# Seven more pairs of expert outputs loaded before the last stage, seven parts instead of six, and gathers without bounds checks, in a graph and mixture-of-experts kernel

## The chip, the cores and the metric

The kernel runs on one core of a Trainium2 chip. The metric is the device time of one execution in microseconds (us). The kernel before takes 3670.58 us (median of three runs, 3669.82 to 3671.08). TensorE multiplies matrices (PE in the profile, PEld its weight loads), VectorE is DVE, ScalarE is ACT, GpSimd is POOL and SyncE, which here only issues DMAs, is SP.

## The reference, cut to what matters

There are 12500 nodes with 256 features each. A first layer sums, for every node, the weighted features of its neighbours over 200,000 sorted edges, and multiplies by a weight matrix. The second layer is the one that the change touches. It scores every node for four experts by attention over 131,072 edges, keeps the two best, and adds up the outputs of four small networks with those gates:

```python
h = (x @ W_gat).reshape(M, HEADS, EXPERTS)
e = leaky_relu(a_src[src] + a_dst[dst], 0.2)      # one value for each edge and head
alpha = exp(e - max over dst) / sum over dst
agg = segment_sum(h[src] * alpha, dst) + b_gat
scores = layernorm(agg, gamma, beta).reshape(M, HEADS, EXPERTS).mean(1)
w = softmax(top_k(scores, 2))
for ei in range(EXPERTS):
    out += gate[ei] * (gelu(x @ W1[ei] + b1[ei]) @ W2[ei] + b2[ei])
```

The result is x plus this sum. The edges of the second layer point at nodes 0 to 8191 only, and every node has a loop to itself.

## The kernel before, in words

The nodes lie in 98 tiles of 128 (`TILES`), and two tiles are a pair (49 pairs). The edges of the second layer are sorted by destination into 128 rows of 1024 columns. The kernel has four stages, each a block in which the five engines run programs of their own, in order, and meet at the end.

`layernorm_and_plan` and `weighted_sums` compute the first layer and sort the edges. Near the end of `weighted_sums`, GpSimd starts to write one small record for each node into `adst_first`, at the node's first edge. That is `spread`, one indirect DMA for each tile (L487): 28 of them are in `weighted_sums` and 70 at the start of the next block. A node without edges has a position far beyond the table, which the DMA's bounds check drops.

`attention_and_experts` does two things side by side. TensorE, ScalarE and a part of VectorE compute the four experts of each pair and store the outputs to `y_dram` (1 MB for a pair, x and the bias already added). GpSimd gathers one record for each edge, 1024 indirect DMAs of 128 rows (L1198), in eight blocks of columns: seven of 140 and the last of 44. For each block VectorE computes running maxima and running sums (`maxima`, `messages`, `sums`), ScalarE the exponentials, and SP stores the states to `state_dram` (L1177). Seven blocks are fitted into slots between pairs, the last comes after the last pair. Then come a short exchange between the 128 rows (`carry`), a gather of one row of states (L1206), its correction and its store (L1209): this is the tail of the softmax. After the states of block 0, SP loads the pairs 0 to 3 into `ys_ahead`, long before they are used. The memset of `m.ns` (L1189) on GpSimd fills the rows of nodes without edges with zeros.

`combine` is the last stage. GpSimd gathers the final state of each node, one indirect DMA for each tile (L1615), in six parts that end at the tiles of `PART`. For a part, VectorE runs the 28 or so small operations of `gates` (L1715 to L1761), with three questions to ScalarE in between (exponential, root, exponential: `weights`, `deviation`, `gate`). Then the pairs of the part are summed. Every fourth pair (every second in the last part) is summed by VectorE (`pair`, L1772 and L1775). The others are summed by TensorE: ScalarE makes eight diagonal matrices of gates (L1644), TensorE multiplies them with the expert outputs (L1686), and ScalarE copies the sum out of PSUM (L1650). ScalarE's order is written out by hand in `summed`: four pairs of part n-1, `weights(n)`, one pair, `deviation(n)`, one pair, `gate(n)`, and the rest. SP first issues the loads of pairs 4 to 15, with three small constant loads among them, and then, in the order of the pairs, stores pair i and refills a slot with pair i-2+16 when the store of pair i-2 has landed. `SLOTS` is 16. SP's DMAs, the state stores of the stage before included, are all on its one queue, q1.

## Time and profile before

| | |
|---|---|
| median of three runs | 3670.58 us |
| the profiled execution | 3668.62 us, its span 3666.8 us |
| TensorE / VectorE / ScalarE / GpSimd busy | 81% / 56% / 22% / 74% of the span |
| mean granted TensorE clock | 0.903 of full speed |
| last stage, first gather to the end of the span | 3488.62 to 3666.8 us |

Times in rows of the trace are microseconds from the start of the span. Busy shares are averages over stages with different limits, so each stage is read by itself. A row of the timeline gives start, duration, engine, line and operation, and in brackets how long the engine was idle before it and what ended that.

### The profile page before, as it was taken

How to read it: one execution, taken by the hardware profiler on the slowest of the kernel's cores; microseconds unless marked ns; L12 is line 12 of the kernel's file. 1: busy time of each engine (PE TensorE's matmuls, PEld its weight loads, DVE VectorE, ACT ScalarE, POOL GpSimd, SP SyncE). 2: the span in 40 equal slices, each digit the busy share in tenths (PEclk: the TensorE clock that was granted, in tenths of full speed). 3: DMA queues.
4: the chain of work that ended last, by engine and by line, in shares of the span. 5: the costliest groups of instructions: out<-in, count | busy, mean ns of one | idle time of the engine just before them, and what ended most of it. 6: DMA issues, size and time to landing. Idle time of an engine off the chain costs nothing. (4 is left out here: it accounts for less than half of the span.)

```text
span 3666.8 us, 60445 instructions
## 1 busy us (share of the span) xinstructions
PE 2973.6 (81%) x13893; PEld 2432.7 (66%) x13894; DVE 2042.9 (56%) x6851; ACT 817.8 (22%) x2321; POOL 2708.2 (74%) x2817
## 2 busy tenths in 40 slices
PE   1475665666866889978888799999999999999648
PEld 1354544554645666766666688888888888888537
DVE  8777778787787676664344223343343334242567
ACT  6300000000111111211222222223232322232247
POOL 6677777777777777777777777777777777777573
PEclk6786887887877999999999899999999999999879
DMA  9643333333433444444444222242223222322289
GB/s 347 198 120 106 107 111 111 112 114 112 116 115 111 121 122 124 128 119 127 128 128 131 58 73 54 54 122 54 73 54 76 54 74 53 79 73 54 57 299 366
DMA packets 276554, 424.71 MB, mean 116 GB/s; under 512 B 59704, under 2 KB 210211, under 8 KB 275363
## 3 DMA queue, kind: packets, MB, share of 16 engines
q0 software_dynamic: 114208, 216.64, 23.6%
q1 hardware_dynamic: 64175, 114.71, 8.6%
q10 hardware_dynamic: 98004, 91.50, 7.7%
q8 instruction: 60, 0.98, 0.1%
q14 instruction: 107, 0.88, 0.1%
HBM read 317.12 MB, written 105.97 MB: 115 GB/s over the span
## 5 line engine op out<-in xcount | busy, mean ns | idle before, releaser
L672 POOL DMA_INDIRECT rows<-feats,src_t x1500 | 1446.8, 965 | 466.9 <-issue 443.6
L1198 POOL DMA_INDIRECT got<-row_dram,src_sorted x1024 | 990.0, 967 | 312.1 <-issue 312.1
L833 PE MATMUL node_sums<-rows,ys_ahead 128*128 x3904 | 989.5, 408 | 231.6 <-SPq L656 101.2
L833 PEld LDWEIGHTS node_sums<-rows,ys_ahead 128*128 128x128 f32 x3904 | 762.4, 202 | 427.5 <-issue 314.9
L1282 PE MATMUL d_hidden<-d_yt,w 128*128 128x256 f32 x3136 | 711.9, 380 | 0.8 <-DVE d_yt L1368 0.8
L1293 PE MATMUL d_expert<-w,hid 128*128 128x256 f32 x3136 | 708.7, 379 | 0.0
L1293 PEld LDWEIGHTS d_expert<-w,hid 128*128 128x128 f32 x3136 | 596.7, 190 | 80.2
L1282 PEld LDWEIGHTS d_hidden<-d_yt,w 128*128 128x128 f32 x3136 | 595.0, 191 | 79.7 <-DVE d_yt L1368 1.2
L1345 DVE TENSOR_TENSOR yo<-d_expert,x_and_b 128x512 f32<-128x512 f32 x196 | 135.5, 691 | 837.5 <-PE d_expert L1293 829.9
L892 DVE TENSOR_SCALAR ys_ahead<-iota,rel,ew_t 128x128 f32<-128x128 f32 x1952 | 557.1, 364 | 65.3 <-DVE rel L888 2.3
L1226 ACT ACTIVATE hid<-d_hidden,b1c 128x256 f32<-128x256 f32 x784 | 323.7, 471 | 983.8 <-PE d_hidden L1282 792.7
L888 DVE TENSOR_SCALAR rel<-dst_t,step_base 128x4 f32 x488 | 123.5, 253 | 508.8 <-PE node_sums L833 421.1
L725 ACT COPY edge_plan<-node_sums 128x256 f32<-128x256 f32 x98 | 36.5, 372 | 1605.2 <-PE sums_and_xc_turned L825 1605.2
L1009 DVE TENSOR_SCALAR ys_ahead<-iota_b,hist_columns 128x128 bf16<-128x128 bf16 (+1 forms) x2048 | 334.5, 279 | 2.5 <-DVE hist_columns L1005 0.2
L845 PE MATMUL counts<-ys_ahead 128*128 128x98 bf16 x1024 | 77.2, 249 | 157.9 <-DVEq L1012 157.9
L845 PEld LDWEIGHTS counts<-ys_ahead 128*128 128x128 bf16 x1024 | 67.8, 122 | 168.1 <-DVEq L1012 165.6
L1615 POOL DMA_INDIRECT edge_plan<-state_dram,last_pos x98 | 100.9, 1029 | 31.9 <-issue 29.6
L487 POOL DMA_INDIRECT adst_first<-node_dst,first_pos x98 | 97.5, 995 | 30.7 <-issue 29.6
L1686 PE MATMUL f_sum<-ys,gate_diagonals 128*128 128x256 f32 x384 | 90.7, 398 | 23.4 <-issue 12.5
L821 PE MATMUL x_product<-edge_plan 128*128 128x256 f32 x400 | 107.1, 392 | 0.0
L1686 PEld LDWEIGHTS f_sum<-ys,gate_diagonals 128*128 128x128 f32 x384 | 76.0, 200 | 38.0 <-issue 27.0
L1418 DVE TENSOR_TENSOR_SCAN got<-decay,last_state,got 128x140 f32<-128x140 f32 (+1 forms) x160 | 86.1, 538 | 4.9
(302 smaller groups left out, 2270.2 us busy)
## 6 DMA issues: line engine op xcount, KB each, us to landing
y_dram<-yo ACTq DMA_DIRECT2D x196, 256.0 KB, 2.2
ys<-y_dram SPq DMA_DIRECT2D x36, 1024.0 KB, 9.2
rows<-feats,src_t POOLq DMA_INDIRECT x1500, 2.8
got<-row_dram,src_sorted POOLq DMA_INDIRECT x1024, 2.4
ys_ahead<-y_dram SPq DMA_DIRECT2D x13, 1024.0 KB, 9.1
x_dram<-edge_plan ACTq DMA_DIRECT2D x98, 128.0 KB
d_x<-x_dram ACTq DMA_DIRECT2D x49, 256.0 KB, 3.1
ys_ahead<-in_x ACTq DMA_DIRECT2D x97, 128.0 KB
```

The source lines that it names most:

```text
L672: pool.indirect_dma_start(rows[:, g % RING, j, :], None, feats, bass.IndirectOffsetOnAxis(ap=m.src_t[:, g * GT + j:g * GT + j + 1], axis=0 ...
L833: t = pe.matmul(psA[:, ds(((code >> 1) & 1) * 512, FEAT)], hot[:, r, j, :], rows[:, ds((code >> 2) & (RING - 1), 1), j, :], start=False, s ...
L845: t = pe.matmul(psC[:, 0:TILES], hot_lo[:, q % 2, j, :], hot_hi[:, q % 2, j, :], start=False, stop=False)
L888: v.tensor_scalar(rel[:, r, :], m.dst_t[:, ds(g * GT, GT)], m.step_base[:, ds(s, 1)], None, ALU.subtract).then_inc(s_rel, 1)
L892: t = v.tensor_scalar(hot[:, r, j, :], m.iota[:], rel[:, r, j:j + 1], m.ew_t[:, ds(g * GT + j, 1)], ALU.is_equal, ALU.mult)
L1009: c.inc(v.tensor_scalar(t[:, q % 2, j, :], iota_b[:, 0:wide], col[:, q % 2, n, j:j + 1], None, ALU.is_equal))
L1198: pool.indirect_dma_start(got[:, k, j, 0:ROWF], None, m.row_dram, bass.IndirectOffsetOnAxis(ap=m.src_sorted[:, BEGIN[b] + j:BEGIN[b] + j + ...
L1226: t = act.activation(hid[:, e % 2, 2 * q + f, :], psL[(e % 2) * 2 + q][:, f, :], ACT.Gelu, bias=b1c[:, e, 2 * q + f:2 * q + f + 1])
L1282: t = pe.matmul(psL[(e % 2) * 2 + q][:, f, :], w1[:, h, e, (2 * q + f) * P:(2 * q + f + 1) * P], yt[:, k, h, :], start=(h == 0), stop=(h = ...
L1293: q = pe.matmul(psO[e % 2][:, t, :], hid[:, e % 2, f, t * P:(t + 1) * P], w2[:, f, e, :], start=(f == 0), stop=(f == FB - 1))
L1345: v.tensor_tensor(yo[:, e, :, :], psO[e % 2][:], xb[:, e, :, :], ALU.add).then_inc(s_yo, 1)
L1686: q = pe.matmul(psum[j % SUMS][:, t, :], diag[:, j % DIAGS, t, e, :], y_of(i)[:, t, e, :], start=(e == 0), stop=(e == EXPERTS - 1))
```

## The change

There are four edits. (1) SP, after it has issued the state store of block 6 and all experts' outputs are stored, loads seven pairs (5 to 11) into memory that the experts no longer need (`w1`, `w2`, `hid`, `yo`, `x_and_b2`). A fifth pair (4) goes early into the free rest of `edge_plan`. `SLOTS` becomes 17, and `combine` itself first loads the three constants and then pairs 12 to 16. (2) `PART` has seven parts instead of six. VectorE takes every third pair of a part, and still every second in the last. (3) The bounds checks of L487 and L1615 are gone. Nodes without edges point at spare rows instead, which SP fills with zeros once in `weighted_sums`. The memset L1189 goes, an iota on GpSimd and three small VectorE operations come in `weighted_sums`. (4) Three semaphores are merged into others.

```diff
-SLOTS = 16
-AHEAD = 4
+SLOTS = 17
+AHEAD = 5
+LATE = 7
...
+        m.y_slots = [m.ys_ahead[:, k] for k in range(AHEAD - 1)] + pairs_of(m.plan[:, TILES * STATE:])
+        for t in (m.w1, m.w2, m.hid, m.yo, m.xb):
+            m.y_slots += pairs_of(t[:].rearrange("p a b c -> p (a b c)"))
...
     pool.indirect_dma_start(m.adst_first, bass.IndirectOffsetOnAxis(ap=m.first_pos[:, t:t + 1], axis=0),
-                            m.node_dst[:, t, :], None, bounds_check=GEDGES - 1, oob_is_err=False
-                            ).then_inc(m.s_sc, 16)
+                            m.node_dst[:, t, :], None).then_inc(m.s_sc, 16)
...
+            c.inc(pool.iota(spare[:], pattern=[[P, TILES]], base=GEDGES, channel_multiplier=1,
+                            allow_small_or_imprecise_dtypes=True))
...
-                c.done(v.tensor_scalar(cnt[:], m.has_edges[:], -4.0 * GEDGES, 4.0 * GEDGES, ALU.mult, ALU.add))
-                c.inc(v.tensor_tensor(m.first_pos[:], pos[:, 0, :], cnt[:], ALU.add))
-                c.done(v.scalar_tensor_tensor(m.last_pos[:], pos[:, 1, :], -1.0, cnt[:], ALU.add, ALU.add))
+                c.inc(v.tensor_tensor(pos[:, 0, :], pos[:, 0, :], spare[:], ALU.subtract))
+                c.done(v.tensor_scalar(pos[:, 1, :], pos[:, 1, :], 1.0, spare[:, 0:1], ALU.subtract, ALU.subtract))
+                c.inc(v.tensor_tensor(pos[:, 0, :], pos[:, 0, :], m.has_edges[:], ALU.mult))
+                c.done(v.tensor_tensor(pos[:, 1, :], pos[:, 1, :], m.has_edges[:], ALU.mult))
+                c.inc(v.tensor_tensor(m.first_pos[:], pos[:, 0, :], spare[:], ALU.add))
+                c.done(v.tensor_scalar(m.last_pos[:], pos[:, 1, :], spare[:, 0:1], None, ALU.add))
...
                     for k in range(AHEAD):
-                        load_pair(sp, m, k, k, m.ys_ahead[:, k])
+                        load_pair(sp, m, k, k, m.y_slots[k])
+                if b == len(BLOCK_PAIR) - 1:
+                    sp.wait_ge(s_l2, PAIRS * EXPERTS)
+                    sp.wait_ge(s_yo, PAIRS * EXPERTS)
+                    for e in range(EXPERTS):
+                        sp.wait_ge(s_st[e], 16 * PAIRS)
+                    for k in range(AHEAD, AHEAD + LATE):
+                        load_pair(sp, m, k, k, m.y_slots[k])
...
-            pool.memset(m.ns, 0.0).then_inc(s_clear, 1)
...
-        PART = [0, 10, 28, 48, 68, 88, T]
+        PART = [0, 6, 18, 36, 56, 74, 90, T]
...
-                     if (i - PART[n] // 2) % (4 if n < PARTS - 1 else 2) == 0]
+                     if (i - PART[n] // 2) % (3 if n < PARTS - 1 else 2) == 0]
...
-            for k in range(AHEAD, SLOTS // 2):
-                load_pair(sp, m, k, k, y_of(k))
             for n, a in enumerate((b_gat, gamma, beta)):
                 sp.dma_start(vec[:, n, :], a.rearrange("(o c) -> o c", o=1).to_broadcast([P, HE])).then_inc(s_c, 16)
-            for k in range(SLOTS // 2, SLOTS):
+            for k in range(AHEAD + LATE, SLOTS):
                 load_pair(sp, m, k, k, y_of(k))
...
-                                            bass.IndirectOffsetOnAxis(ap=m.last_pos[:, t:t + 1], axis=0),
-                                            bounds_check=GEDGES - 1, oob_is_err=False).then_inc(s_got[part], 16)
+                                            bass.IndirectOffsetOnAxis(ap=m.last_pos[:, t:t + 1], axis=0)
+                                            ).then_inc(s_got[part], 16)
```

## Rows read from the trace of the kernel before

**Rows 1.** The page, what the DMA engines moved in 40 slices of 91.7 us.

```profile
GB/s 347 198 120 106 107 111 111 112 114 112 116 115 111 121 122 124 128 119 127 128 128 131 58 73 54 54 122 54 73 54 76 54 74 53 79 73 54 57 299 366
```

**Rows 2.** The timeline of POOL around the end of the spreads.

```profile
2154.36 0.97 POOL L487 DMA_INDIRECT adst_first<-node_dst,first_pos  x1 [0.30 <-issue]
2155.32 2.09 POOL L1189 MEMSET edge_plan<- 128x2352 f32 x1
2157.57 1.00 POOL L1190 DMA_INDIRECT adfirst<-adst_dram,dst_first  x1 [0.16 <-issue]
```

**Rows 3.** The timeline of the softmax's tail: SP, POOL and DVE.

```profile
3453.26 23.40 SPq L1177 DMA_DIRECT2D state_dram<-got  x2
...
3459.72 0.94 POOL L1198 DMA_INDIRECT got<-row_dram,src_sorted  x1 [0.30 <-issue]
...
3462.12 0.18 DVE L1389 TENSOR_SCALAR limit<-seg_keep 128x44 f32<-128x44 f32 x1 [8.95 <-DMA got<-row_dram,src_sorted]
...
3476.08 0.18 DVE L1422 COPY last_state<-got 128x20 f32<-128x20 f32 x1
...
3479.80 0.94 POOL L1206 DMA_INDIRECT first_row<-state_dram,first_end  x1 [19.14 <-DMA state_dram<-got]
...
3483.16 0.16 DVE L1510 TENSOR_TENSOR row_max<-first_row,in_max 128x4 f32<-128x4 f32 x1
```

**Rows 4.** DMA issues from 3350 us on: count, KB each, median us to landing.

```profile
ys<-y_dram SPq DMA_DIRECT2D x36, 1024.0 KB, 9.2
...
out<-ys SPq DMA_DIRECT2D x36, 256.0 KB, 8.9
...
state_dram<-got SPq DMA_DIRECT2D x1, 1680.0 KB, 5.6
...
state_dram<-got SPq DMA_DIRECT2D x1, 528.0 KB, 2.6
```

**Rows 5.** Waits from 3487 us on: us in total, times, longest.

```profile
DVE f_w L1715 <- DMA edge_plan<-state_dram,last_pos: 15.2, 5, 5.1
...
DVE num L1721 <- ACT f_w L1625: 7.9, 6, 3.9
```

**Rows 6.** The timeline of DVE in the last stage.

```profile
3506.41 0.20 DVE L1715 TENSOR_TENSOR f_w<-edge_plan,one 128x40 f32<-128x40 f32 x1 [2.49 <-DMA edge_plan<-state_dram,last_pos]
...
3515.98 0.74 DVE L1772 TENSOR_SCALAR ys_ahead<-ys_ahead,sc 128x256 f32<-128x256 f32 x2 [0.16 <-DVE sc L1761]
...
3519.76 0.73 DVE L1772 TENSOR_SCALAR ys<-ys,sc 128x256 f32<-128x256 f32 x2
...
3526.95 0.23 DVE L1715 TENSOR_TENSOR f_w<-edge_plan,one 128x72 f32<-128x72 f32 x1 [3.26 <-DMA edge_plan<-state_dram,last_pos]
...
3539.27 0.74 DVE L1772 TENSOR_SCALAR ys<-ys,sc 128x256 f32<-128x256 f32 x2 [0.16 <-DVE sc L1761]
...
3556.32 0.24 DVE L1715 TENSOR_TENSOR f_w<-edge_plan,one 128x80 f32<-128x80 f32 x1 [5.14 <-DMA edge_plan<-state_dram,last_pos]
...
3569.36 0.86 DVE L1772 TENSOR_SCALAR ys<-ys,sc 128x256 f32<-128x256 f32 x2 [0.16 <-DVE sc L1761]
...
3651.18 0.62 DVE L1772 TENSOR_SCALAR ys<-ys,sc 128x256 f32<-128x256 f32 x2 [0.16 <-DVE sc L1761]
```

**Rows 7.** The timelines of POOL, PE and ACT in the last stage.

```profile
3488.62 1.02 POOL L1615 DMA_INDIRECT edge_plan<-state_dram,last_pos  x1 [2.30 <-POOLq L1088]
...
3500.36 0.99 POOL L1615 DMA_INDIRECT edge_plan<-state_dram,last_pos  x1 [0.30 <-issue]
...
3518.51 12.36 PE L1686 MATMUL f_sum<-ys_ahead,gate_diagonals 128*128 128x256 f32 x48 [35.59 <-ACT gate_diagonals L1644]
...
3524.00 0.58 ACT L1650 COPY ys_ahead<-f_sum 128x512 f32<-128x512 f32 x1 [3.30 <-PE f_sum L1686]
...
3663.07 0.58 ACT L1650 COPY ys<-f_sum 128x512 f32<-128x512 f32 x1 [2.87 <-PE f_sum L1686]
```

**Rows 8.** A window: length, busy PE, PEld, DVE, ACT, POOL; PEclk, DMA share, GB/s.

```profile
3518.00:3521.00 3.00, 2.50 (x6) 2.08 (x7) 2.82 (x7) 2.70 (x10) 2.37 (x3) 0.50 1.02 412
```

More of the change, by code:

```diff
@@ L128, in build @@
         m.s_store = [sem(f"tile_stored{k}") for k in range(SLOTS)]
-        layers = top.enter_context(ExitStack())
-        def weights(name, shape):
-            return layers.enter_context(nc.sbuf_tensor(name, shape, F32))
         m.plan = keep("edge_plan", [P, 3 * ECOLS])
         m.ns = m.plan[:, 0:TILES * STATE].rearrange("p (t c) -> p t c", c=STATE)
-        m.ys_ahead = keep("ys_ahead", [P, AHEAD, 2, EXPERTS, FEAT])
-        m.w1 = weights("w1", [P, HALVES, EXPERTS, HID])
-        m.w2 = weights("w2", [P, FB, EXPERTS, FEAT])
-        m.b1c = weights("b1c", [P, EXPERTS, FB])
-        m.b2r = weights("b2r", [P, EXPERTS, FEAT])
+        m.ys_ahead = keep("ys_ahead", [P, AHEAD - 1, 2, EXPERTS, FEAT])
+        m.w1 = keep("w1", [P, HALVES, EXPERTS, HID])
+        m.w2 = keep("w2", [P, FB, EXPERTS, FEAT])
+        m.b1c = keep("b1c", [P, EXPERTS, FB])
+        m.b2r = keep("b2r", [P, EXPERTS, FEAT])
         with ExitStack() as part1:
@@ L162, in build, with pairs_of @@
             weighted_sums(nc, sem, feats, edge_index, x, W, b, W_gat, att_src, att_dst, W1, b1, W2, b2, m)
+        m.hid = keep("hid", [P, 2, FB, N2])
+        m.yo = keep("yo", [P, EXPERTS, 2, FEAT])
+        m.xb = keep("x_and_b2", [P, EXPERTS, 2, FEAT])
+        def pairs_of(flat):
+            n = 2 * EXPERTS * FEAT
+            return [flat[:, a:a + n].rearrange("p (t e f) -> p t e f", e=EXPERTS, f=FEAT)
+                    for a in range(0, flat.shape[1] - n + 1, n)]
+        m.y_slots = [m.ys_ahead[:, k] for k in range(AHEAD - 1)] + pairs_of(m.plan[:, TILES * STATE:])
+        for t in (m.w1, m.w2, m.hid, m.yo, m.xb):
+            m.y_slots += pairs_of(t[:].rearrange("p a b c -> p (a b c)"))
+        assert len(m.y_slots) == AHEAD + LATE
         attention_and_experts(nc, sem, m)
-        layers.close()
         combine(nc, sem, b_gat, gamma, beta, out, m)
@@ L313, in _ @@
             pool.memset(m.eps[:], LN_EPS).then_inc(s_const, 1)
-            pool.memset(xlast[:], 0.0).then_inc(s_clear, 1)
+            pool.memset(xlast[:], 0.0).then_inc(s_raw0, 1)
             pool.iota(m.iota[:], pattern=[[1, P]], base=0, channel_multiplier=0,
@@ L384, in scale @@
                 v.wait_ge(s_std, n + 1)
-                v.reciprocal(rstd[:, k, :], rstd[:, k, :]).then_inc(s_rcp, 1)
-                v.wait_ge(s_rcp, n + 1)
+                c.done(v.reciprocal(rstd[:, k, :], rstd[:, k, :]))
                 v.scalar_tensor_tensor(shift[:, k, :], mv[:, k, :, 0], -1.0, rstd[:, k, :], ALU.mult, ALU.mult
@@ L551, in weighted_sums @@
         tot = lent(TILES)
+        spare = lent(TILES)
         pos = lent(2 * TILES).rearrange("p (n t) -> p n t", n=2)
@@ L606, in weighted_sums @@
                     cur = 1 if cur == 2 else 1 - cur
-        PC = 13
+        PC = 14
         @block.sync
@@ L652, in _ @@
                     sp.dma_start(flat[k - (RING - 8)], zeros[:]).then_inc(s_zo, 16)
+            sp.dma_start(m.state_dram[GEDGES:GEDGES + P, :], zeros[:, 0:STATE]).then_inc(s_zo, 16)
             with sp.Fori(2, full_rounds) as i:
@@ L703, in _ @@
             pool.wait_ge(s_pos, 1)
-            pool.wait_ge(s_zo, 16 * 8)
+            pool.wait_ge(s_zo, 16 * 9)
             pool.wait_ge(s_row, 1)
```

28 lines of the change are left out of this document (11 added, 17 removed).

## The prediction

> **What bounds the kernel now.** I read the page first, then the timeline of each engine in the last 220 us, then the waits and DMA issues of that stretch. The DMA engines move 54 to 131 GB/s until the last two slices, where they move 299 and 366 [rows 1]. So only the end can be short of transfers, and there the page alone suggests a DMA bound. The timeline says otherwise. A load of a pair lands 9.2 us after its issue [rows 4], and with 16 slots it is issued so early that the summing never waits for one: in the waits of that stretch the engines wait for gathers and for each other [rows 5], not for y_dram. What sets the end is a chain through VectorE. The first part's gathers land at 3506.41; then gates, the part's vector pairs, the wait for the next part's gathers, and gates again, up to the last gates at 3651.18 [rows 6]; then TensorE's last pairs and the stores. In numbers, before: 3506.4 + 77.8 (six gates) + 54.2 (14 vector pairs) + 12.7 (the four later gather waits, the 15.2 of rows 5 less the first, 2.5) = 3651.1, which is the row. Within the gates 7.2 us are waits for ScalarE beyond the shortest round trips: 77.8 against 70.6 for the same sizes undisturbed.
>
> Before that stage lies the softmax's tail. Its last block starts when GpSimd's last gather has landed (start 3459.72, landed 3462.12, 2.40 us), its states are computed by 3476.3, stored, and read back by GpSimd at 3479.80; VectorE needs that row at 3483.16 [rows 3]. GpSimd is never idle from the first spread on, so what is taken from its queue moves this tail.
>
> **The edits outside the last stage.** The memset takes 2.09 + 0.16 us of GpSimd's queue [rows 2]: -2.25 for its last gather. A spread is 0.97 long with the bounds check, an edge gather without it 0.94 [rows 2, 3]. But the scatter and gather differ otherwise too, as the unchecked L1190 at 1.00 shows [rows 2]. So 98 spreads are worth 0 to 98 x 0.03 = 2.9 us; I take the middle, 1.4. The iota (a fraction of a us), the zeros, the three VectorE operations and the semaphores lie in `weighted_sums`, where GpSimd waits for ring slots in its beginning; I cost them at nothing, and at 1 us if that cover is gone. The last gather then starts at 3459.7 - 3.7 = 3456.0.
>
> Against this stand the seven loads, issued behind the store of block 6 at 3453.26. The last gathers now land among them. A gather among loads took 3500.36 to 3506.41, 6.05 us [rows 6, 7], against 2.40 alone: +3.65. So the last block starts at 3462.1: no change, between -5.1 (no cost from the loads, all of the spreads) and +1.4. Next, the last state store. The store of block 6 takes 5.6 us [rows 4]; seven loads are 7.34 MB, at the 412 GB/s of a stretch full of them [rows 8] 17.8 us, at the 366 of the last slice [rows 1] 20.1. From the end of that store, 3458.9, they end at 3476.7 to 3479.0, beside the store's issue at 3476.3. Alone it lands in 2.6 us; a small store among loads takes 8.9 [rows 4]. With the loads nearly over I take the low end plus a bit, 3.5, as now. Tail: 0, ends -4 and +6.
>
> What this row shows has a rule beside it. The Trainium skill, DMA: Bandwidth & Descriptors, section Queues, rings and completion order, says that the descriptors of SP's queue are consumed in ring order on each DMA engine. By that rule the last state store would wait for every load still unfinished in front of it, which speaks against this edit; it is the second rival's mechanism.
>
> The bounds check on L1615 is worth about 0.05 x 98 = 5 us of GpSimd (1.30 from one gather to the next, against 1.25 for the edge gathers), but the chain takes it only where VectorE waits for gathers.
>
> **The last stage, step by step.** Prices [rows 6]: gates of 10, 18 and 20 tiles take 9.57 (3506.41 to 3515.98), 12.32 and 13.04 us, so 0.344 a tile, and 8.2, 10.3, 11.6 and 8.9 for 6, 12, 16 and 8 tiles. A vector pair takes 3.78, with later ones up to 4.0; I take 3.86. A tensor pair needs 2.5 us of diagonals, then 5.5 on TensorE if it is the first after an idle time (3518.51 to 3524.00 [rows 7]), where the granted clock is 0.50 [rows 8], which is 1.2 GHz, and 3.45 if not (the other 6.9 of the 12.36 us for three pairs).
>
> - Part 0 (6 tiles): sixth gather at 3488.62 + 5 x 1.25 = 3494.9, five loads still run, + 6.05 = 3500.9. That is 5.5 earlier than now. Gates done 3509.1, one vector pair to 3512.9.
> - Part 1 (12 tiles): gathers landed 3512.3. But ScalarE's order puts `weights(1)` behind both tensor pairs' diagonals and the copy of the first: 3509.1 + 2.5 + 5.5 + 0.6 = 3517.7. VectorE waits 4.1. Gates done 3527.4, two vector pairs to 3535.
> - Part 2 (18): the 36th gather starts at 3532.7, lands about 3538.8: wait 3.8. ScalarE gets to `weights(2)` after the third of the four tensor pairs (restarted at the low clock, 3530 + 5.5 + 2 x 3.45 + 0.6 = 3543.0): 3.4 more. Gates done 3554.5; three vector pairs to 3566.1.
> - Part 3 (20): the same again, `weights(3)` after three pairs from a restart at 3557: 3.0. Done 3582.1; four vector pairs to 3597.5.
> - Part 4 (18): no wait, done 3609.8; three pairs, 3621.4. Part 5 (16): ScalarE is behind by 1.6, done 3634.6; three pairs, 3646.2. Part 6 (8): 1.6, done 3656.9.
>
> In sum: 3500.9 + 76.6 (seven gates) + 13.7 (ScalarE) + 3.9 (gathers) + 61.8 (16 vector pairs) = 3656.9. After it come two tensor pairs: 2.6 + 6.9 + 0.2 + 0.6 + 3.1 (copy end to span end, 3663.65 to 3666.8 now [rows 7]) = 13.4, so 3670.3. Against 3666.8 that is +3.5. By terms: earlier start -5.5, gates +6.0, ScalarE +6.5, gathers -8.8, two more vector pairs +7.6, a shorter end -2.3. TensorE has one pair less, 31 for 32, and is not the bound. The preloaded pairs themselves are worth nothing here, since loads are waited for neither before nor after; their cover is the 17 slots, and if the loads fell behind, the end would go with them at 2.6 us a pair.
>
> The ScalarE term is the least sure. Its low end is about 5 less (no slow restarts, 2.1 in each of two, and a little order), its high end some 4 more. The first part's landing can be 3.65 less. So the last stage gives -5 to +8.
>
> The profiled execution took 3668.62, the median is 3670.58. With +3.4 and a tail of 0 I get 3670.6 + 3.4 = 3674.0.
>
> **Rivals.** *The disturbance ends, and the time falls.* The earlier loads leave the DMA queues free, so the gathers land in 2.40 instead of 6.05 in the first part (-3.65), the tail takes all of GpSimd's gain, about -4, and the slow restarts of TensorE don't recur (-4.2). 3674.0 - 11.9 = 3662.1. For it: the gathers' wait is 15.2 us now. Against it: five loads are still issued at the stage's start. Half of it would stay within 0.2%.
>
> *The last state store queues behind the seven loads (slower).* It lands 8.9 after its issue like an output store, not 2.6: +6.3, less 1 us by which VectorE is later than that row now. 3674.0 + 5.3 = 3679.3. It decides if loads are still running at about 3476, when VectorE ends block 7. For it: my two rates put their end at 3476.7 and 3479.0.
>
> *The late loads do not start early.* If SP's waits for the last expert stores held it until the store of block 7, GpSimd's gain would be free of them (-3.7), and twelve loads would meet the first gathers as now: about 3670. Against it: the experts' stores are long landed by 3453.
>
> **How the numbers follow.** The forecast, with a last stage within some 5 us of +3.4, has 0.50. The first rival has 0.22, the second 0.18, the third 0.10. A measurement of this kernel can tell about 0.2%, 7.3 us, from no change: 3663.2 to 3677.9. The forecast's own spread leaks a little on both sides. So faster 0.25, same 0.52, slower 0.23. The range takes the first rival and the second with its spread: 3661 to 3681.
>
> **What would show it.** Right: the last stage starts within 2 us of now; first gates about 3501; VectorE's wait for `weights` exceeds 7.9 us clearly; seven gates sum to 88 to 92 us; last gates about 3657 from a start at 3488. Wrong: VectorE's wait for ScalarE at or below now's, first-part gathers landing in 3 us, GpSimd reading the row back well before or after 3479.8, or any engine waiting for a pair's load.

## The result, and the profile after

The changed kernel takes **3680.14 us** (median of 11 runs, 3674.59 to 3683.45), the kernel before, on the same chip, 3669.82 (11 runs, 3666.54 to 3672.62). The ratio is 1.0024, its 95% interval 1.0016 to 1.0031: slower, by 10.3 us between the medians and 8.8 by the ratio. The forecast was 3674.0, 3.4 above before. The time lies in the range, 0.9 us inside its upper end, and on the side to which 0.23 had been given.

The profiled execution took 3681.55 us (before 3668.62), and its span is 3679.6 (3666.8). Four readings of it matter. First the hand-over from the softmax to the last stage, in the timelines of SP, POOL and DVE of the changed kernel (start, length, engine and line, and in brackets the idle time before and what ended it):

```profile
3456.56 0.32 SPq L1185 DMA_DIRECT2D state_dram<-got  x1
3457.13 4.37 SPq L1092 DMA_DIRECT2D w<-y_dram  x4
...
3463.30 2.61 SPq L1092 DMA_DIRECT2D x_and_b<-y_dram  x1
3463.74 0.95 POOL L1212 DMA_INDIRECT got<-row_dram,src_sorted  x1 [0.30 <-issue]
3468.95 0.19 DVE L1402 TENSOR_SCALAR limit<-seg_keep 128x44 f32<-128x44 f32 x1 [12.47 <-DMA got<-row_dram,src_sorted]
...
3483.19 0.34 SPq L1185 DMA_DIRECT2D state_dram<-got  x1
...
3486.58 0.95 POOL L1219 DMA_INDIRECT first_row<-state_dram,first_end  x1 [21.90 <-issue]
...
3495.39 0.97 POOL L1626 DMA_INDIRECT edge_plan<-state_dram,last_pos  x1 [2.19 <-POOLq L1099]
```

The seven loads go out at 3457.13 to 3465.9, right behind the store of block 6, as the diff says. The last edge gather, started at 3463.74, is used at 3468.95, 5.21 later; before it was 2.40 [rows 3]. The last stage's first gather starts at 3495.39, 6.8 later than the 3488.62 of [rows 7], and from there to the end of the span it is 184.2 us, for 178.2 before.

Part of the 6.8 is this execution's own. Its first spread starts at 2032.88, 4.6 later than before, in a stretch that the change hardly touches, while that of the same kernel, run again, starts at 2029.10, 0.8 later. From the first spread to the last edge gather it is 1430.86 us here, 0.6 less than the 1431.45 before, and the gather's landing adds 2.8: 4.6 - 0.6 + 2.8 = 6.8. GpSimd's instructions were a little longer in this execution than when the same kernel ran again (a spread 991 ns for 982, an edge gather 968 for 966, 1024 of them), which took back most of what the change gives its queue. The second execution is therefore the better measure of the hand-over, and the first experiment gives it.

Second, VectorE in the last stage. Of parts 0 and 2 the line at which it takes up the part, of parts 1 to 3 the one at which ScalarE's `weights` let it go on, and of parts 0 and 6 the first vector pair, which is the end of their gates:

```profile
3507.68 0.18 DVE L1726 TENSOR_TENSOR f_w<-edge_plan,one 128x24 f32<-128x24 f32 x1 [8.20 <-DMA edge_plan<-state_dram,last_pos]
...
3516.17 0.74 DVE L1783 TENSOR_SCALAR ys_ahead<-ys_ahead,sc 128x256 f32<-128x256 f32 x2 [0.16 <-DVE sc L1772]
...
3526.04 0.36 DVE L1732 TENSOR_TENSOR num<-edge_plan,f_w 128x192 f32<-128x192 f32 x1 [5.34 <-ACT f_w L1636]
...
3545.66 0.23 DVE L1726 TENSOR_TENSOR f_w<-edge_plan,one 128x72 f32<-128x72 f32 x1 [2.43 <-DMA edge_plan<-state_dram,last_pos]
3551.23 0.46 DVE L1732 TENSOR_TENSOR num<-edge_plan,f_w 128x288 f32<-128x288 f32 x1 [4.73 <-ACT f_w L1636]
...
3578.17 0.49 DVE L1732 TENSOR_TENSOR num<-edge_plan,f_w 128x320 f32<-128x320 f32 x1 [3.35 <-ACT f_w L1636]
...
3664.91 0.61 DVE L1783 TENSOR_SCALAR x_and_b<-x_and_b,sc 128x256 f32<-128x256 f32 x2 [0.16 <-DVE sc L1772]
```

Third, the waits from 3487 us on (us in total, times, longest):

```profile
DVE num L1732 <- ACT f_w L1636: 17.9, 7, 5.3
...
DVE f_w L1726 <- DMA edge_plan<-state_dram,last_pos: 10.6, 2, 8.2
```

The two waits have changed places. For gathers VectorE waited 15.2 us, now 10.6, of which 8.2 are the first part's; for ScalarE 7.9, now 17.9 [rows 5]. No engine waits for a pair. One wait of before stands in no row so far, VectorE's for the three small constants, which were queued behind four pair loads:

```profile
DVE vec L1700 <- DMA vec<-in_L_ffn_ln_beta: 14.0, 1, 14.0
```

Now the constants go first, and that wait is 2.9. With ten tiles in the first part the gathers landed later still, so it cost nothing then; experiment 3 shows where it would.

Fourth, why ScalarE is late: TensorE in the same stretch.

```profile
3518.69 9.97 PE L1697 MATMUL f_sum<-ys_ahead,gate_diagonals 128*128 128x256 f32 x32 [28.92 <-ACT gate_diagonals L1655]
3538.07 5.37 PE L1697 MATMUL f_sum<-edge_plan,gate_diagonals 128*128 128x256 f32 x16 [9.41 <-ACT gate_diagonals L1655]
...
3564.63 5.74 PE L1697 MATMUL f_sum<-yo,gate_diagonals 128*128 128x256 f32 x16 [10.83 <-issue]
...
3586.57 3.69 PE L1697 MATMUL f_sum<-ys_ahead,gate_diagonals 128*128 128x256 f32 x16 [2.30 <-issue]
3592.36 8.83 PE L1697 MATMUL f_sum<-ys_ahead,gate_diagonals 128*128 128x256 f32 x32 [2.10 <-issue]
...
3667.39 8.83 PE L1697 MATMUL f_sum<-ys,gate_diagonals 128*128 128x256 f32 x32 [4.91 <-issue]
```

The trace has each product as two records, and sixteen records are one pair. After 9.4 and 10.8 us of idleness a pair takes 5.4 to 5.7 us, after 2.3 it takes 3.69. The last two pairs follow 4.91 us of idleness and take 8.83, and so do the two at 3592.36, after only 2.10; at their best two take 7.14 (an experiment below shows such a row). A slow first pair after a gap is called a slow restart below. It is the granted clock, in windows over such stretches (length, busy PE, PEld, DVE, ACT, POOL, then PEclk, DMA share and GB/s):

```profile
3532.00:3538.00 6.00, 0.00 (x0) 0.00 (x0) 5.17 (x20) 2.76 (x10) 4.58 (x5) 0.50 0.13 10
3538.00:3543.00 5.00, 4.92 (x15) 4.15 (x16) 4.68 (x11) 2.76 (x9) 3.78 (x5) 0.65 0.74 217
3586.00:3590.00 4.00, 3.44 (x16) 2.96 (x16) 3.35 (x13) 2.67 (x6) 2.85 (x4) 1.00 1.03 376
```

TensorE idles from 3532 to 3538 and is granted 0.50, the level of 1.2 GHz; in its next five microseconds it has 0.65 on the mean; around 3586 it has 1.00, the level of 2.4 GHz. From 3592 to 3594 it has 0.67, and 0.60 from 3667 to 3671, where the last two pairs begin.

### The profile page after: what moved, and what is told of

Its sections match the earlier page's. It is cut to its first block and busy times, and to the rows that moved or that the text cites. A ratio compares the mean times of both kernels' runs of the same rounds, so it can differ in the third digit from the quotient of the medians.

```text
span 3679.6 us, 60264 instructions
## 1 busy us (share of the span) xinstructions
PE 2977.6 (81%) x13877; PEld 2432.8 (66%) x13878; DVE 2052.8 (56%) x6894; ACT 820.0 (22%) x2317; POOL 2708.6 (74%) x2817
## 5 line engine op out<-in xcount | busy, mean ns | idle before, releaser
L829 PEld LDWEIGHTS x_product<-edge_plan 128*128 128x128 f32 x400 | 79.2, 198 | 11.7
L336 POOL DMA_INDIRECT rows<-in_x,src_t x64 | 61.9, 967 | 33.9 <-issue 19.2
```

Of the source, the lines that this page charges most:

```text
L829: t = pe.matmul(psX[:, 0:FEAT], sums_t[:, k * P:(k + 1) * P], w_t[:, k, :], start=False, stop=(k == HALVES - 1))
```

## The experiments

Experiments 1 to 4 ran on one chip and 5 to 8 on another. The kernel before took 3670.15 us on the first and 3670.01 on the second, so their times are set side by side. Experiments 9 to 12 ran on a third chip, of which more below.

**1. The changed kernel again**, to part what belongs to the kernel from what belongs to one execution. No edit.

> The changed kernel once more, for its trace beside others of the same chip. In its first trace the last gather of edges starts 4.0 us later than before, although a 2.25 us memset is gone, and every indirect DMA of GpSimd is about 4 ns longer (949 against 946 ns in the median). Theory A (the added time before the tail belongs to the kernel): again 3679 to 3682 us, with gathers of 949 ns. Rival B (it belongs to the execution): the times spread from 3674 to 3683, and a trace with gathers of 944 to 946 ns is 5 to 6 us shorter.

Measured: 3680.87 us (3672.80 to 3685.52), ratio 1.0024 (1.0015 to 1.0033) to 3670.15 for the kernel before. The last gather starts at 3457.05, 2.7 earlier than in [rows 3], and is used at 3464.24, 2.1 later:

```profile
3464.24 0.19 DVE L1402 TENSOR_SCALAR limit<-seg_keep 128x44 f32<-128x44 f32 x1 [10.00 <-DMA got<-row_dram,src_sorted]
```

From the first spread to that gather it is 1427.95 us, for 1431.45 before: GpSimd's queue gave 3.5 back, the predicted 3.65. The loads take more than that away: the landing went from 2.40 to 7.19. The last stage begins at 3490.71, 2.1 later than before, and lasts 189.3 us, five more than in the first profile. TensorE's rows differ from the first profile's in three slow restarts, and VectorE's show what came of them:

```profile
3583.12 5.36 PE L1697 MATMUL f_sum<-ys_ahead,gate_diagonals 128*128 128x256 f32 x16 [2.31 <-issue]
...
3616.68 15.74 PE L1697 MATMUL f_sum<-ys,gate_diagonals 128*128 128x256 f32 x64 [2.06 <-issue]
...
3643.20 5.38 PE L1697 MATMUL f_sum<-edge_plan,gate_diagonals 128*128 128x256 f32 x16 [2.02 <-issue]
```

```profile
3629.83 0.43 DVE L1732 TENSOR_TENSOR num<-edge_plan,f_w 128x256 f32<-128x256 f32 x1 [3.48 <-ACT f_w L1636]
...
3656.30 0.29 DVE L1732 TENSOR_TENSOR num<-edge_plan,f_w 128x128 f32<-128x128 f32 x1 [3.56 <-ACT f_w L1636]
```

The first profile has 3.69, 14.05 and 3.69 for the three. After waits of equal length, 2.0 to 2.3 us, the first pair is now 1.67 to 1.69 us longer; TensorE had been busy throughout from 3576.0 to 3580.8 at a granted clock of 1.00, and after 2.3 us of idleness it has 0.50 from 3583.1 to 3586.0. The second and the third stand in ScalarE's queue ahead of `weights(5)` and `weights(6)`, for which VectorE now waits 3.48 and 3.56 us, where it waited 1.80 and 1.88: the same 1.68 each. The one at 3583 comes after `weights(3)` in that queue, and the first profile has one of its own at 3592.36, where this one has 7.15; neither delays VectorE, whose wait for `weights(4)` is 0.45 in both. The rest of the five are 1.1 more for `weights(3)`, 1.3 more for the gathers of part 2 and 0.5 at the end, less 0.7 for `weights(1)`. VectorE's wait for ScalarE is 21.5 in sum. So the slow restarts differ from execution to execution, and where VectorE stands behind one, so does the time. That this is why the 11 runs spread over 12.7 us is likely and not shown: only one of them has a trace.

**2. The changed kernel with the old parts.** Late loads and gathers without checks stay.

```diff
-        PART = [0, 6, 18, 36, 56, 74, 90, T]
+        PART = [0, 10, 28, 48, 68, 88, T]
...
-                     if (i - PART[n] // 2) % (3 if n < PARTS - 1 else 2) == 0]
+                     if (i - PART[n] // 2) % (4 if n < PARTS - 1 else 2) == 0]
```

> The changed kernel with six parts and every fourth pair on VectorE, as before. Theory: the seven parts cost 6 us of the added 10 in the last stage (weights waits for ScalarE 17.9 instead of 7.9 us, two more vector pairs in VectorE's chain), so 3674 us, 6 below the changed kernel, and the span from the first gather of the last stage to the end is about 178 instead of 184. Rival: the parts are neutral and the seven loads in the tail cost it all; then 3680 as the changed kernel.

Measured: 3668.54 us (3667.00 to 3672.50), ratio 0.9996 (0.9987 to 1.0005). The new parts cost 12.3 us in this company (10.0 between the means of the runs). The last stage is 175.9 long from its first gather, and the two waits stand the other way round again:

```profile
DVE f_w L1726 <- DMA edge_plan<-state_dram,last_pos: 22.7, 5, 12.6
DVE num L1732 <- ACT f_w L1636: 9.5, 6, 3.9
```

**3. The new parts alone, on the kernel before.** The same two lines the other way round; one semaphore of the first stage is saved, as in the change, for the seventh part's.

> The kernel before with the new parts and every third pair on VectorE alone. Theory: +5 to +6 us on the kernel before, 3675 to 3676, all of it after the first gather of the last stage. Rival (the parts only pay with twelve pairs loaded ahead): more than that, since the slots run dry; or, if the parts are neutral, 3670.

Measured: 3678.87 us (9 runs, 3677.77 to 3682.89), ratio 1.0027 (1.0017 to 1.0037): +8.7. It has none of the late loads and none of the saved checks. VectorE waits 18.4 us for `weights`. So the parts alone carry nearly the whole of what the change costs. One thing in it belongs to this company. The constants are still queued behind four pair loads here, and with six tiles in the first part it is they, and not the gathers, that VectorE waits for:

```profile
3504.83 0.17 DVE L1699 TENSOR_SCALAR vec<-vec 128x16 f32<-128x16 f32 x1 [15.14 <-DMA vec<-in_L_ffn_ln_beta]
```

It takes up part 0 16.2 us after the stage's first gather, for 12.3 in the changed kernel. So up to 4 us of the 8.7 are the constants' place (an estimate from these two rows). From there to the end of the span it is 170.9 us, for 160.4 before and 171.9 in the changed kernel: that part of the loss is the parts' own.

**4. The changed kernel without the late loads.** The block in SP's program goes, and its seven pairs are loaded at the beginning of the last stage instead (`range(AHEAD, SLOTS)` for `range(AHEAD + LATE, SLOTS)`).

> The changed kernel with pairs 5 to 16 all loaded by the last stage itself, no loads in the softmax's tail. Theory: the last edge gathers land in 2.4 instead of 5.2 us, and nothing in the last stage waits for a pair, so 2.8 us less than the changed kernel, 3677. Rival 1 (the preloading pays in the last stage): slower than the changed kernel by up to 5 us. Rival 2 (the loads in the tail cost nothing): the same time.

Measured: 3673.20 us (3669.80 to 3679.09), ratio 1.0011 (1.0002 to 1.0020), 7.7 less than the changed kernel in experiment 1 (5.1 between the means). The tail, against experiment 1:

```profile
3461.02 0.19 DVE L1395 TENSOR_SCALAR limit<-seg_keep 128x44 f32<-128x44 f32 x1 [6.38 <-DMA got<-row_dram,src_sorted]
```

The last gather started at 3457.44 and is used 3.58 later, not 7.19; the last stage starts 3.2 earlier, at 3487.46. It is then 183.7 long, as in the first profile, with 15.1 of waits for ScalarE. That the pairs come 31 us later than in the changed kernel delays nothing, and the first part's gathers, with twelve loads issued beside them in place of five, land 12.6 us after the stage's first gather, for 12.3.

**5. Neither late loads nor new parts.** Both edits undone: what is left is the gathers and spreads without checks, the memset gone, 17 slots, the constants ahead of the pairs, and the merged semaphores.

> The changed kernel with the old parts and without the loads in the tail: what is left is the removed bounds checks and memset, and 17 slots. Theory (the tail follows GpSimd's queue, and the late loads cost the last gathers' landing some 2 to 3 us): 2 to 4 us less than the kernel before, 3666 to 3668, and 1 to 3 less than the variant with old parts and late loads (3668.5). Rival 1 (the late loads pay with the old parts): slower than 3668.5. Rival 2 (the removed checks and memset are worth nothing): 3670.

Measured: **3663.90 us** (3662.49 to 3668.56), ratio 0.9984 (0.9975 to 0.9993) to 3670.01 for the kernel before. It is 6.1 us faster than before and 16 to 17 faster than the whole change. Its last gather is used at 3461.11 and the last stage starts at 3487.53.

With experiments 1, 2 and 4 this makes a square (medians, us):

| | old parts | new parts | new parts cost |
|---|---|---|---|
| no late loads | 3663.90 | 3673.20 | 9.3 |
| late loads | 3668.54 | 3680.87 | 12.3 |
| late loads cost | 4.6 | 7.7 | |

By the means of the same runs the new parts cost 9.8 and 10.0, and the late loads 4.9 and 5.1. The runs of experiment 1 lie in two groups, five from 3672.80 to 3677.62 and six from 3680.87 to 3685.52, and its median is the lowest of the upper one. So the two costs are shown, of some 10 and some 5 us, but not that each is dearer beside the other.

**6. ScalarE asks earlier.** If VectorE's wait comes from the place of `weights(n)` in ScalarE's hand-written order, it must fall when `weights(n)` goes before the fourth tensor pair. The change stays whole, parts and loads.

```diff
-                summed(n - 1, 0, 4)
+                summed(n - 1, 0, 3)
                 weights(n)
-                summed(n - 1, 4, 5)
+                summed(n - 1, 3, 4)
                 deviation(n)
-                summed(n - 1, 5, 6)
+                summed(n - 1, 4, 5)
                 gate(n)
-                summed(n - 1, 6, PAIRS)
+                summed(n - 1, 5, PAIRS)
```

> The changed kernel with ScalarE's order shifted by one pair: weights after three pairs of a part instead of four, deviation after four, gate after five. Theory (the seven parts lose because VectorE waits for ScalarE at weights): the wait of VectorE's first multiplication for ScalarE's exponential falls from about 20 to under 15 us, and the time by some 5 us, to 3676. Rival (that wait only covers for another, such as TensorE's pairs): the time stays at 3680.

Measured: 3668.47 us (3667.61 to 3670.73), ratio 0.9996 (0.9987 to 1.0005). No computation is added or left out, and 12.4 us are gone against experiment 1 (10.3 between the means). So is the spread: 3.1 us over 11 runs, for 12.7.

```profile
DVE f_w L1726 <- DMA edge_plan<-state_dram,last_pos: 12.7, 3, 8.2
DVE num L1732 <- ACT f_w L1636: 7.6, 7, 4.9
```

The slow restarts are still there (one pair in 5.38 us after 2.29 idle), and it is here that the last two pairs take 7.14:

```profile
3575.82 5.38 PE L1697 MATMUL f_sum<-ys,gate_diagonals 128*128 128x256 f32 x16 [2.29 <-issue]
...
3657.57 7.14 PE L1697 MATMUL f_sum<-ys,gate_diagonals 128*128 128x256 f32 x32 [1.84 <-issue]
```

They no longer matter much, because VectorE doesn't stand behind them.

**7. TensorE kept busy.** The other half of the same chain: the order stays, and slow restarts are taken away by products whose result nobody uses, put into four of TensorE's waits. (The line that allocates their PSUM tensor is not shown.)

```diff
+                for _ in range({0: 44, 2: 19, 6: 22, 29: 9}.get(j, 0)):
+                    pe.matmul(idle_ps[:], m.ones[:], m.node_row[:].rearrange("p t c -> p (t c)")[:, 0:FEAT],
+                              start=True, stop=True)
```

> The changed kernel with matrix products of no use (44, 19, 22 and 9 of 128x256, into a PSUM bank of their own) placed into four idle times of TensorE in the last stage: before its first pair, before the first pairs of parts 1 and 2, before those of the last part. Theory (TensorE starts each part at the low clock, which costs 1.7 to 3.0 us a restart, and the number of such restarts makes the executions of the changed kernel differ by 10 us): first pairs of 3.5 instead of 5.4 to 6.7 us, a time 5 to 8 us less, 3673 to 3676, and a narrower spread. Rival 1 (the clock is not what sets the chain): no change. Rival 2 (the products outlast the idle times): slower by what they outlast.

Measured: 3670.45 us (3668.26 to 3673.51), ratio 1.0002 (0.9993 to 1.0011): 10.4 less than the changed kernel in experiment 1 (8.8 between the means), with 94 products more. In the rows `f_idle` are the 44 first useless products, then come the stage's first two pairs and its last two:

```profile
3488.91 21.37 PE L1693 MATMUL f_idle<-node_row,ones 128*128 128x256 f32 x88 [5.01 <-PEq L1099]
3513.20 8.83 PE L1701 MATMUL f_sum<-ys_ahead,gate_diagonals 128*128 128x256 f32 x32 [2.92 <-ACT gate_diagonals L1656]
...
3656.86 7.14 PE L1701 MATMUL f_sum<-ys,gate_diagonals 128*128 128x256 f32 x32 [1.02 <-issue]
```

The last two are back at 7.14. The first two take 8.83, less than the 9.24 of experiment 1 and the 9.97 of the first profile, but not 7.14: TensorE still idled 2.92 before them. The first pairs of parts 1 and 2 take 3.69 each, and VectorE's waits for `weights(2)` and `weights(3)` fall to 1.1 and 0.9. Its wait for ScalarE is 10.7 in sum. One slow restart more is left, at 3581.87, where nobody waits for it.

**8. Every third pair alone**, on the kernel of experiment 5 (`% 3` with the old parts).

> The variant with the checks removed, the old parts and no late loads, with every third pair of a part on VectorE instead of every fourth. Theory (the share of VectorE is neutral, the number and size of the parts is what costs): within 3 us of that variant. Rival (the bigger share of VectorE costs through VectorE's chain): 4 to 8 us slower than it.

Measured: 3664.81 us (3663.35 to 3666.77), ratio 0.9988 (0.9979 to 0.9997). Against experiment 5 that is +0.9, too little to be told from nothing. So of the 9.3 that the new parts cost, the share of `% 3` taken alone is small, and the cut of the parts (or the two together) has the rest.

**Experiments 9 to 12** ran together on the third chip, where the kernel before itself took 6078.32 us (29 runs, mean granted clock 0.73); their ratios are to it, and they are not set against the eight above. The times that the expectations name are those of the first two chips, so none of them could come true there.

**9. Bounds checks back**, on the kernel of experiment 5.

```diff
-                            m.node_dst[:, t, :], None).then_inc(m.s_sc, 16)
+                            m.node_dst[:, t, :], None, bounds_check=GEDGES + NPAD - 1, oob_is_err=False
+                            ).then_inc(m.s_sc, 16)
...
-                                            bass.IndirectOffsetOnAxis(ap=m.last_pos[:, t:t + 1], axis=0)
-                                            ).then_inc(s_got[part], 16)
+                                            bass.IndirectOffsetOnAxis(ap=m.last_pos[:, t:t + 1], axis=0),
+                                            bounds_check=GEDGES + P - 1, oob_is_err=False).then_inc(s_got[part], 16)
```

> The variant with old parts and no late loads (3663.9), with bounds checks put back on both indirect DMAs, at limits that nothing exceeds; the memset stays away. Theory (of its 6 us, 2.3 are the memset and the rest the checks): a spread is 0.97 long with the check and a gather of the last stage 1.00 instead of 0.95, so the last stage's gathers come up to 5 us later, and 2 to 4 us are lost, 3666 to 3668. Rival (the checks lie beside other work): 3664.

Measured: 6073.32 us, ratio 0.9991 (0.9981 to 1.0001; one of the 12 runs took 7779.13 and is not in the ratio). What the checks are worth in time was not settled, since experiment 5 has no run on that chip. Their price in the queue was: the groups of POOL with checks (the mean of one in ns is the last number before the second bar),

```profile
L1620 POOL DMA_INDIRECT edge_plan<-state_dram,last_pos x98 | 99.4, 1015 | 31.8 <-issue 29.5 <-POOLq L1100 2.3
L492 POOL DMA_INDIRECT adst_first<-node_dst,first_pos x98 | 97.3, 992 | 105.3 <-DVEq L1062 67.2 <-issue 29.2 <-POOLq L509 8.9
```

and without them, in experiment 10 on the same chip:

```profile
L1620 POOL DMA_INDIRECT edge_plan<-state_dram,last_pos x98 | 93.5, 954 | 31.8 <-issue 29.6 <-POOLq L1099 2.2
L492 POOL DMA_INDIRECT adst_first<-node_dst,first_pos x98 | 96.0, 979 | 105.1 <-DVEq L1061 66.6 <-issue 29.3 <-POOLq L508 9.2
```

A gather of the last stage pays 61 ns for its check, a spread 13: 6.0 and 1.3 us for 98 of each. In the kernel before the same means were 1029 and 995 ns, in experiment 5 976 and 984.

**10. TensorE kept busy, old parts**: experiment 5 with 58 useless products before the first pair and 22 before the fourth.

> The same variant (3663.9) with products of no use in TensorE's two long idle times of the last stage, 58 before the first pair, 22 before the first pair of part 1. Theory (two restarts at the low clock of 1.7 to 2.6 us each are in its chain): 1 to 4 us less, 3660 to 3663. Rival (with the old parts VectorE waits for gathers behind these, so a faster restart is lost in that wait): 3664.

Measured: 6098.47 us, ratio 1.0034 (1.0020 to 1.0048; one of the 12 runs took 13388.62 and is not in the ratio): slower than the kernel before on that chip. Its trace has the loss in the last stage, which lasts 278.1 us from its first gather, for 258.8 in experiment 9. From 5842 on TensorE's instructions come one at a time, the useless products first: 0.4 to 0.6 us each, mostly with 2.2 us between them, until about 5958. Why they come so slowly the trace doesn't say. So what the products are worth when they fill idle time alone was not measured here.

**11. Order, products and parts together**, without late loads (experiment 4 with the order of experiment 6 and 76 useless products).

> The seven parts with what the runs so far showed to help: no loads in the tail, ScalarE's order one pair earlier, and products of no use in three idle times of TensorE (44, 19 and 13). Theory (the three losses of the changed kernel add up: 12.4 for ScalarE's order, 7.7 for the late loads, and part of 10.4 for the clock): 3658 to 3662, below both kernels and below 3663.9. Rival (they overlap, since each shortens the same chain): 3663 to 3668.

Measured: 6103.23 us (6 runs), ratio 1.0046 (1.0030 to 1.0062); its last stage lasts 280.6 us. Neither of the two says anything of the chips of the first eight, where no run was faster than experiment 5. Whether the order of experiment 6 adds to experiment 5 there wasn't tried.

**12. The late loads later still**, on experiment 2: SP holds the seven loads until ScalarE has been asked for the last block (a wait on `s_go`), so that they are under way when the last state store is issued.

```diff
                     for e in range(EXPERTS):
                         sp.wait_ge(s_st[e], 16 * PAIRS)
+                    sp.wait_ge(s_go, BLOCKS)
                     for k in range(AHEAD, AHEAD + LATE):
```

> The variant with old parts and late loads (3668.5), where SP starts the seven loads only after the last block's maxima, so that no edge gather lands among them, but the last state store stands behind more of them. Theory (the late loads cost through the gathers' landing): the last edge gathers land in 3.6 us as without late loads; the store then takes up to 8.9 us to land instead of 2.6, so 0 to 4 us slower than 3668.5 although the gathers are 2 to 3 us faster. Rival (the queue is no matter): 3665 to 3666.

Measured: 6095.64 us, ratio 1.0029 (1.0017 to 1.0041). What it was made for stands in rows: SP and DVE in its tail, and the same store in its DMA issues (KB, us to landing).

```profile
5805.40 2.32 SPq L1092 DMA_DIRECT2D w<-y_dram  x4
...
5815.94 0.34 SPq L1185 DMA_DIRECT2D state_dram<-got  x1
...
5828.46 0.94 POOL L1220 DMA_INDIRECT first_row<-state_dram,first_end  x1 [343.31 <-DMA state_dram<-got]
...
5830.97 0.16 DVE L1524 TENSOR_TENSOR row_max<-first_row,in_max 128x4 f32<-128x4 f32 x1 [8.24 <-DMA first_row<-state_dram,first_end]
```

```profile
state_dram<-got SPq DMA_DIRECT2D x1, 528.0 KB, 11.8
```

The store lands after 11.8 us, GpSimd reads the row at 12.5 after its issue, and VectorE, which had waited for nothing here in experiment 10 on the same chip, waits 8.24. In experiment 10, without late loads, the same store lands in 2.6, and so it does in the changed kernel:

```profile
state_dram<-got SPq DMA_DIRECT2D x1, 528.0 KB, 2.6
```

What the DMA engines moved from 3440 to 3500 in the changed kernel, in slices of 1.5 us, shows how close it was:

```profile
GB/s 13 176 14 7 7 26 169 7 7 182 7 249 332 430 150 344 408 362 389 415 401 412 412 404 415 399 412 164 3 273 87 0 8 0 0 8 0 10 79 302
```

The loads fill the slices up to 3480.5 and a part of the next; cut finer, they end at about 3481.1, and the store is issued at 3483.19. In experiment 1 it is closer: 430 GB/s from 3477 to 3478 and 164 in the next microsecond, with the store issued at 3478.49, which landed in 2.9.

## Why the prediction was right or wrong

**The chain was read rightly.** VectorE sets the end through gates, its own pairs and its waits; no engine waits for a pair; the preload is worth nothing, as the terms said. Experiment 4 shows it from the other side: taken away, the late loads give back 7.7 us (5.1 between the means). The direction was right as well.

**GpSimd's queue**: -3.65 predicted to the last edge gather, -3.5 measured in experiments 1 and 5, counted from the first spread (experiment 5: 3457.58 less 2029.60 = 1427.98, for 1431.45). The memset went as priced. The spreads gave 995 less 982 ns each in experiment 1, 1.3 in sum, for the 1.4 taken.

**The tail: 0 predicted, +6.8 in the first profile, +2.1 in experiment 1, and -1 without the loads.** The landing of the last gathers among loads was priced at 6.05 from a gather in [rows 6, 7]; it measured 5.2 in the first profile, 5.6 in experiment 2, 7.2 in experiment 1. So of the +2.1 the landing is 1.1, and 0.8 is that the first spread starts later. The work added to `weighted_sums`, costed at nothing, may have a part in that: the first spread starts at 2028.3 and 2028.4 in the two traces without it (before and experiment 3) and at 2027.6 to 2030.0 in experiments 1, 2 and 4 to 8, which does not part the two. And the offset against GpSimd's gain left out that the landing grows even without loads: in experiments 4 and 5 the last gather, started 2.1 to 2.3 us earlier, takes 3.5 to 3.6, not 2.40, so that only 1.1 of the gain arrives at the last stage. In experiment 5 it starts 2.7 us after the issue of block 6's store, before it started 6.5 after; that the two meet is likely the reason, but was not tried. "No change, between -5.1 and +1.4" was thus too kind: at +2.1 (experiment 1) it is beyond that end, though within the +6 that the whole tail was given. The first profile's +6.8 is beyond that too, but 4.6 of it came before the first spread.

**The last stage: +3.5 predicted, +6.0 in the first profile, +11.1 in the second.** Counted from the stage's first gather, step by step:

| | predicted | first profile | experiment 1 |
|---|---|---|---|
| part 0 landed | 12.3 | 12.3 | 12.3 |
| gates 0 done | 20.5 | 20.8 | 20.8 |
| gates 1 | 38.8 | 40.2 | 39.4 |
| gates 2 | 65.9 | 66.8 | 67.3 |
| gates 3 | 93.5 | 94.5 | 95.7 |
| gates 4 | 121.2 | 122.3 | 123.5 |
| gates 5 | 146.0 | 147.1 | 150.0 |
| gates 6 | 168.3 | 169.5 | 174.1 |
| end | 181.7 | 184.2 | 189.3 |

The landing of part 0, which had been given a low end of 3.65 less, is right to the tenth. The term that came out too small is the **ScalarE term**. Its places were right: parts 1 to 3 and 5, 6. VectorE's waits for `weights` are 15.1 beyond the shortest round trips in the first profile (17.9 less seven of 0.4), for the 13.7 worked out; in experiment 1 they are 18.7. Counted as the prediction counts it, all that seven gates take beyond their undisturbed 76.6, the term is 17.1 and 20.7, since the gates sum to 93.7 and 97.3 us. The other terms in the same order, predicted, first profile, experiment 1: gathers 3.9, 2.4, 3.8; sixteen vector pairs 61.8, 61.1, 60.8; the end 13.4, 14.7, 15.2. So of the 2.5 and 7.6 us by which the stage is longer than forecast, 3.4 and 7.0 are the ScalarE term and 1.3 and 1.8 the end, while the gathers and the pairs took a little less than forecast.

The forecast carried a slow restart for the first tensor pair of parts 0, 1 and 2, at 5.5 us, and left all later pairs and the last two at the full clock: "3.45 if not" the first after idleness. Parts 1 and 2 restarted in 5.4 to 6.7 us. Experiment 1 has three slow restarts more, each 1.7 us, after waits of 2.0 to 2.3 us; two of them stand in ScalarE's queue ahead of a `weights` that VectorE waits for, and these two cost it 3.4. And the last two pairs took 8.83 or 9.39, not 6.9, after TensorE had been idle for 4.9 us.

Experiments 6 and 7 show that both halves of that chain are needed for the loss. Moving `weights` ahead of one pair gives 12.4 us with the restarts in place; taking most of the restarts away gives 10.4 with the order in place. Together that would be more than the new parts cost, so the two overlap: they shorten one wait from two sides. Both changes in one kernel ran only on the third chip. Experiment 3 shows that the wait comes with the parts and not with the loads.

The kernel before has slow restarts as well, but VectorE seldom stands behind them: it waits for the gathers of a larger part (15.2 us against 7.9 for ScalarE), and its 11 runs spread over 6.1 us only (its 31 and 33 later ones over 9.8 and 6.6). By making the first parts small the change hid the gathers, as it was to, and put a longer wait in their place. The Trainium skill, TensorE: Matmul & The Clock Gate, section What's actually happening, says that the ramp costs under 1% of a typical kernel and that the number of slow matmuls varies from run to run. The traces agree with both: the 10 us that experiment 7 gave back are 0.3% here, and the three restarts above differ between two executions of one kernel. But 0.3% is all that is at stake in this change.

**The forecast's own margin.** The sum is 6.8 + 6.0 = +12.8 in the first profile and 2.1 + 11.1 = +13.2 in experiment 1, and +10.3 and +10.7 in medians, for +3.4. The last stage's range of "-5 to +8" ended below the second profile. That the time lies in the range is in part luck: the forecast's own terms were some 7 us short, and the range reached to 3681 because it took in the second rival, whose mechanism was not there.

**The signs that had been named.** VectorE's wait for `weights` exceeds 7.9 clearly, and no engine waits for a pair's load: these came true. The last stage starts 6.8 and 2.1 us later than before, not within 2; the first gates are at 3507.7 and 3503.0, not 3501; seven gates sum to 93.7 and 97.3, not 88 to 92. And one sign of being wrong is there: GpSimd reads the row back at 3486.58 and 3482.12, not at 3479.8. The tail, and the size of the ScalarE term, are what was wrong.

**The rivals.** *The disturbance ends, and the time falls* (3662.1): false. The first part's gathers took the same 12.3 with seven pairs already loaded; five loads were still issued there, and with all twelve (experiment 4) it was 12.6, so the number of loads hardly mattered. The slow restarts recurred, and there were more. But its number is nearly that of experiment 5, 3663.9, which has GpSimd's gain without the late loads and the new parts.

*The last state store queues behind the seven loads* (3679.3): its time is the one measured, and its mechanism was not there. The store landed in 2.6 us in the first profile, where the loads had ended some 2 us before it was issued, and in 2.9 in experiment 1, where they were just ending. The two rates put the loads' end at 3476.7 to 3479.0, which was right (about 3478.4 in experiment 1); the store, set at 3476.3, was issued at 3478.49, 2.2 later, as the whole last block came 2.1 later. Experiment 12 shows the mechanism when the loads are still running: 11.8 us, for the 8.9 of the prediction. The Trainium skill, DMA: Bandwidth & Descriptors, section Queues, rings and completion order, has descriptors consumed in ring order on each DMA engine; experiment 12's row agrees with that, and the changed kernel escapes it by 2 us in one execution and by next to nothing in the other. A forecast that had put its weight on this rival would have hit the time for a wrong reason.

*The late loads do not start early* (3670): false, they were issued at 3457.13, 0.6 after the store of block 6.

**What stays open.** How the 6.1 us of experiment 5 divide among the memset, the checks of the spreads, those of the last stage's gathers, the slots and the constants' place. By rows 1.1 arrive at the stage's beginning and 1.9 in it (176.3 for 178.2), 3.0 of the 6.1; the other 3 are that the profiled execution of before was 1.4 us below its median here and that of experiment 5 1.7 above its own. Also open is how much of the new parts' cost belongs to the cut alone, since `% 3` was undone alone on the old parts only.

## What to carry to other kernels

Where two engines hand work to and fro in an order written out by hand, a new tiling needs a new order: after cutting the parts, look at what stands in the feeding engine's queue ahead of the thing that the critical engine asks for, and move that first (here 12.4 us, 10.3 by the means, for four lines). A transfer that nobody waits for gains nothing by starting earlier and can cost something, since what it then runs beside may be on the chain. And when a change is a bundle, measure its parts: here two edits cost 16 to 17 us, and what is left without them was worth 6.

## What the runs showed of the hardware

- A TensorE pair that follows only 2.0 to 2.3 us of idleness takes 3.69 us in one execution and 5.36 to 5.38 in another of the same kernel, at the same place. In the slow case the granted clock is 1.00 over the 4.8 us in which it was busy before the gap and 0.50 for the 2.9 us after it. The kernel's run-to-run spread was 12.7 us where VectorE stood behind such pairs (experiment 1) and 3.1 where it did not (experiment 6). But in experiment 3, where VectorE waits 18.4 us for ScalarE, it was 5.1 over 9 runs, so one need not follow from the other.
- 44 useless products in an idle stretch, and 50 more in three others, made the kernel 10.4 us faster (8.8 between the means). On the third chip, where such products came one at a time with 2.2 us between them, the last stage was 19 us longer with them.
- A store of 528 KB took 2.6 us alone and 11.8 behind seven loads of 1 MB on the same queue (both on one chip); a gather on GpSimd's own queue beside such loads took 5.2 to 7.2 us instead of 2.4 to 3.6.
- The bounds check of an indirect DMA took 61 ns of GpSimd on a gather (1015 for 954, 98 of each) and 13 on a scatter (992 for 979).
